# Second layer's products in column halves, behind the first layer's and in a projection bank, with two score banks in the last stage

## What is computed

```python
# layer 0: 20 heads of 64
n = layer_norm(x);  x = x + attention(n, n, a1)            # self-attention
n = layer_norm(x);  x = x + attention(n, ctx, a2)          # over 77 rows of context
x = geglu_ff(layer_norm(x)) + x
# layer 1: 20 heads of 8; text = ctx[:, :-4], ip = ctx[:, -4:]
q = heads(x @ W_q)
probs_t  = softmax(q @ heads(text @ W_k).T * s)            # 128 x 73 a head
text_out = probs_t @ heads(text @ W_v)
qsem  = l2norm(probs_t @ text);  sem = qsem @ l2norm(ip).T
fused = q @ heads(ip @ W_k_ip).T * s + 0.5 * sem
ip_out = (softmax(fused) * fside) @ heads(ip @ W_v_ip)
out = (text_out + ip_out) @ W_out + b_out + x
```

## Time and profile before

| | us |
|---|---|
| runs shown | 3484.98 median, 3480.99 to 3485.95 |
| the profiled execution | 3485.28 |
| its span | 3483.4 |
| TensorE, matmuls busy | 3335.4 (96%) |
| TensorE, weight loads busy | 3131.8 (90%) |
| DVE busy | 2438.3 (70%) |
| ACT busy | 2314.2 (66%) |
| POOL busy | 1329.5 (38%) |

### The profile page before, as it was taken

The page is one execution under the profiler, slowest core; times in us unless marked ns, Lnnn a source line. Parts: engine busy times, 40 slices in busy tenths (PEclk is TensorE's granted clock), DMA queues, the critical chain, the costliest instruction groups (busy, mean ns, idle before and its releaser), DMA issues. The chain is left out here.

```text
span 3483.4 us, 96098 instructions
## 1 busy us (share of the span) xinstructions
PE 3335.4 (96%) x34878; PEld 3131.8 (90%) x34878; DVE 2438.3 (70%) x7677; ACT 2314.2 (66%) x6485; POOL 1329.5 (38%) x1657
## 2 busy tenths in 40 slices
PE   5899999999999999999999999999999999999997
PEld 4789999999899999999999899998999999899987
DVE  6657677767767767677767767767677776777655
ACT  4566676766767676676766767676676766767654
POOL 2223343333434433343433434433343333434333
PEclk9999999999999999999999999999999999999998
DMA  6432324223142332324223142332324223142310
GB/s 157 157 116 69 105 63 126 74 86 103 54 123 70 108 90 68 108 63 122 78 83 105 54 123 68 106 94 63 113 64 118 82 82 106 54 124 68 94 51 11
DMA packets 210732, 313.84 MB, mean 90 GB/s; under 512 B 31232, under 2 KB 167520, under 8 KB 210272
## 3 DMA queue, kind: packets, MB, share of 16 engines
q1 hardware_dynamic: 209984, 307.53, 30.5%
q10 hardware_dynamic: 288, 0.16, 0.0%
HBM read 267.97 MB, written 14.42 MB: 81 GB/s over the span
## 5 line engine op out<-in xcount | busy, mean ns | idle before, releaser
L997 ACT ACTIVATE SE<-PS,mx 128x77 f32<-128x77 f32 (+1 forms) x2560 | 674.8, 355 | 271.9 <-DVE mx L1248 271.2
L1461 POOL TENSOR_TENSOR SE<-SE,rs 128x512 f32<-128x512 f32 (+1 forms) x640 | 552.7, 869 | 625.7 <-DVE rs L1270 625.7
L1454 POOL TENSOR_TENSOR n<-qq,p_half 128x4 f32<-128x4 f32 x320 | 327.4, 1023 | 987.0 <-DVE qq L1299 987.0
L1265 DVE TENSOR_REDUCE sums<-SE 128x4 f32<-128x512 f32 (+1 forms) x640 | 368.3, 576 | 217.8 <-ACT SE L997 217.3
L985 ACT ACTIVATE PTs<-PT 128x1024 f32<-128x1024 f32 (+1 forms) x320 | 326.5, 1020 | 242.3 <-PE PT L811 240.7
L933 ACT ACTIVATE qk<-PG 128x512 f32<-128x512 f32 (+1 forms) x640 | 326.3, 510 | 127.2 <-PE PG L612 125.5
L773 PE MATMUL PW<-w_o,OTs 128*128 128x160 f32 x2560 | 408.8, 303 | 0.0
L1248 DVE TENSOR_REDUCE mx<-PS 128x8 f32<-128x1024 f32 (+1 forms) x320 | 323.0, 1010 | 115.6 <-PE PS L793 113.4
L827 PE MATMUL PV<-PTs,v_sb 128*64 128x128 f32 (+1 forms) x5120 | 351.1, 279 | 12.3 <-DVE SE L1291 12.0
L773 PEld LDWEIGHTS PW<-w_o,OTs 128*128 128x128 f32 x2560 | 359.7, 191 | 0.0
L876 PE MATMUL PV<-later 73*128 73x86 f32 x2560 | 331.0, 272 | 2.3 <-ACT later L1006 1.4
(11 more groups left out here) (209 smaller groups left out, 8439.1 us busy)
## 6 DMA issues: line engine op xcount, KB each, us to landing
q_slice<-q_split SPq DMA_DIRECT2D x630, 192.0 KB, 2.4
vc_slice<-vc_split SPq DMA_DIRECT2D x155, 512.0 KB, 4.0
kc_slice<-kc_split SPq DMA_DIRECT2D x150, 256.0 KB, 2.9
q1st<-q_hi SPq DMA_DIRECT2D x320, 32.0 KB, 2.1
k1st<-k_hi SPq DMA_DIRECT2D x160, 38.5 KB, 2.2
xres<-in_x_dram SPq DMA_DIRECT2D x32, 160.0 KB, 2.7
q1st<-q_lo SPq DMA_DIRECT2D x160, 32.0 KB, 2.1
out_dram<-x SPq DMA_DIRECT2D x64, 80.0 KB, 1.6
```

Source lines behind the costliest of these rows:

```text
L997: last = a_(SE[:, n % 4, J * i:J * i + J], PS[:, e, J * at:J * at + J], ACT.Exp, bias=mx[:, q % 2, 4 * e + at:4 * e + at + 1])
L1265: v.tensor_reduce(sums[:, n % 2, :], SE[:, n % 4, 0:4 * J].rearrange("p (i j) -> p i j", j=J), AX, ALU.add)\
L1454: gp.tensor_tensor(n20[:, b % 2, 4 * w:4 * w + 4], qq[:, b % 2, 4 * w:4 * w + 4], p_half[:, 0:4], ALU.pow)\
L1461: gp.tensor_tensor(e, e, rs[:, n % 2, :].unsqueeze(2).to_broadcast([128, 4, J]), ALU.mult)\
```

## The change

Four things are changed together. The products of a unit (`probs_v1`) are split in two halves of 64 rows of output, so that 4 matmuls of 128 columns of weights become 8 of 64, written to partitions 0 to 63 and 64 to 127. They are no longer issued in part 2 of the beat behind the unit, but in part 0 of the beat after that, directly behind `probs_v`. They no longer go to `PV` but are a job, `pv1`, first in its step, with a bank of `PG` that `unit_out` frees; the semaphore `pv1_done` goes, and `probs_v` and `probs_v1` don't wait for each other's readers. `unit_out` moves on DVE from the end of the beat to sub 0 behind `softmax_in`, `unit_norms` from there to sub 1 behind the first `prob_sums`, `norms_of` on POOL to sub 1 behind the normalisations. The tail's steps start one step later and its jobs stand at the same steps as before. In the last stage (`alone`) the scores of every second unit go to a bank of `PS`, and the scores are issued ahead of the transposes.

```diff
-    TAIL_JOB = {"ipT": 7, "ip": 10, "oT1": 13, "y": 16}
+    TAIL_JOB = {"ipT": 6, "ip": 9, "oT1": 12, "y": 15}
...
-            return 3 * l1_beat(g, W1 * b + W1 - 1) + 7
+            return 3 * l1_beat(g, W1 * b + W1 - 1) + 8
+
+        def alone(g, k):
+            return l1_beat(g, k) > DUOS * GROUPS + 1
+
+        def scores1_bank(g, k):
+            return PS[:, 0, :] if alone(g, k) and k % 2 else PT[:, 1, :]
...
+            unit = l1_at(t // 3 - 2) if t % 3 == 0 else None
+            products1 = [("pv1",) + unit] if unit else []
...
-            return first + v, [x for x in late_at(t) if x[0] != "v"]
+            return products1 + first + v, [x for x in late_at(t) if x[0] != "v"]
...
-                        "ctx1": "gv_done", "ipT": "ipT_done", ...
+                        "ctx1": "gv_done", "pv1": "on_done", "ipT": "ipT_done", ...
...
 # probs_v
-                    if product1[0]:
-                        pe.wait_ge(S["on_done"], product1[0])
 # scores1
-                    if j > 1:
+                    if alone(g, k - 1):
+                        pe.wait_ge(S["exp1_done"], j - 2)
+                        pe.wait_ge(S["exp_done"], NL0 * GROUPS)
+                    elif j > 1:
                         pe.wait_ge(S["exp1_done"], j - 1)
...
-                    mm(PT[:, 1, 0:4 * T], q1st[...],
+                    mm(scores1_bank(g, k)[:, 0:4 * T], q1st[...],
...
 # probs_v1
+                    name = ("pv1", g, k)
+                    pe.wait_ge(*read_out(JOBS[JOB[name] - len(PG)]))
                     pe.wait_ge(S["pts1_done"], j)
-                    if multiplied:
-                        pe.wait_ge(S["ots_done"], multiplied)
-                    if j > 1:
-                        pe.wait_ge(S["on_done"], j - 1)
...
-                        last = mm(PV[:, GV * i + off:GV * i + off + GS + D1], PTs1[0:TT, 128 * i:128 * i + 128],
-                                  gv[:, b % 2, 2 * w + i // 2, off:off + GS + D1], start=True, stop=True)
-                    last.then_inc(S["pv1_done"], 1)
-                    product1[0] = j
+                        for c in range(2):
+                            last = mm(bank(name)[64 * c:64 * c + 64, GV * i + off:GV * i + off + GS + D1],
+                                      PTs1[0:TT, 128 * i + 64 * c:128 * i + 64 * c + 64],
+                                      gv[:, b % 2, 2 * w + i // 2, off:off + GS + D1], start=True, stop=True)
+                    last.then_inc(S["job_full"], 1)
...
 # TensorE's steps
                         if duo_at(beat - 1):
                             probs_v(*duo_at(beat - 1))
+                        if l1_at(beat - 2):
+                            probs_v1(*l1_at(beat - 2))
+                    ahead = part == 1 and l1_at(beat) and alone(*l1_at(beat))
+                    if ahead:
+                        scores1(*l1_at(beat), turned)
                     if part == 1 and l1_at(beat - 1):
                         probs_transposed1(*l1_at(beat - 1), turned)
-                    if part == 1 and l1_at(beat):
+                    if part == 1 and l1_at(beat) and not ahead:
                         scores1(*l1_at(beat), turned)
...
-                    if part == 2 and l1_at(beat - 1):
-                        probs_v1(*l1_at(beat - 1), multiplied)
...
 # DVE's steps
                     if sub == 0 and l1_at(beat - 2):
-                        unit_norms(*l1_at(beat - 2))
+                        unit_out(*l1_at(beat - 2))
...
                         prob_sums(g, 2 * d)
+                    if sub == 1 and l1_at(beat - 2):
+                        unit_norms(*l1_at(beat - 2))
...
-                    if sub == 2 and l1_at(beat - 1):
-                        unit_out(*l1_at(beat - 1))
...
 # POOL's steps
-                    if sub == 0 and l1_at(beat - 2):
+                    if sub == 1 and l1_at(beat - 2):
                         norms_of(*l1_at(beat - 2))
```

More of the change, by code:

```diff
@@ L462, in read_out @@
                         "down": "down_added", "q1": "q1_done", "k1": "k1_done", "vip": "vip_done",
-                        "ctx1": "gv_done", "ipT": "ipT_done", "ip": "o1_done", "oT1": "o1T_done", "y": "y_done"}
+                        "ctx1": "gv_done", "pv1": "on_done", "ipT": "ipT_done", "ip": "o1_done", "oT1": "o1T_done", "y": "y_done"}
             return S[freed_by[name[0]]], NTH[name]
@@ L485, in wait_gv_used @@
                 if g0 >= 0:
-                    engine.wait_ge(S["pv1_done"], l1_count(g0, W1 * b0 + W1 - 1))
+                    engine.wait_ge(S["job_full"], JOB[("pv1", g0, W1 * b0 + W1 - 1)] + 1)
             @block.sync
@@ L875, in probs_v1 @@
                         off = D1 * (i % 2)
[L876 to L879 removed]
+                        for c in range(2):
[3 more added lines that the diff above has]
+                    last.then_inc(S["job_full"], 1)
                 for t in range(FIRST, LAST):
                     beat, part = divmod(t, 3)
[L883 removed]
+                    turned = min(max(beat + 1, 0), DUOS * GROUPS)
                     if part == 0:
@@ L890, in _ @@
                             probs_v(*duo_at(beat - 1))
+                        if l1_at(beat - 2):
[3 more added lines that the diff above has]
+                        scores1(*l1_at(beat), turned)
                     if part == 1 and l1_at(beat - 1):
                         probs_transposed1(*l1_at(beat - 1), turned)
-                    if part == 1 and l1_at(beat):
+                    if part == 1 and l1_at(beat) and not ahead:
                         scores1(*l1_at(beat), turned)
                     for name in jobs_at(t)[0]:
-                        job(name)
+                        if name[0] != "pv1":
+                            job(name)
                     if part == 1 and beat > DUOS * GROUPS and l1_at(beat):
                         keep_busy(6)
-                    if part == 2 and l1_at(beat - 1):
-                        probs_v1(*l1_at(beat - 1), multiplied)
                     for name in late_at(t):
@@ L1004, in pt1_out @@
                     if j > 1:
-                        act.wait_ge(S["pv1_done"], j - 1)
+                        act.wait_ge(S["job_full"], JOB[("pv1",) + divmod(j - 2, GB * W1)] + 1)
                     a_(PTs1[0:TT, :], PT[0:TT, 0, :], ACT.Copy).then_inc(S["pts1_done"], 1)
@@ L1014, in exp1 @@
                     for i in range(4):
-                        last = a_(SE1[:, j % 2, TT * i:TT * i + TT], PT[:, 1, T * i:T * i + TT], ACT.Exp,
+                        last = a_(SE1[:, j % 2, TT * i:TT * i + TT], scores1_bank(g, k)[:, T * i:T * i + TT], ACT.Exp,
                                   bias=mx1[:, j % 2, i:i + 1])
@@ L1274, in unit_out @@
                     j = l1_count(g, n)
-                    dve.wait_ge(S["pv1_done"], j)
+                    ps = take(("pv1", g, n))
                     b, w = n // W1, n % W1
-                    o = PV[:, 0:4 * GV].rearrange("p (i d) -> p i d", d=GV)
+                    o = ps[:, 0:4 * GV].rearrange("p (i d) -> p i d", d=GV)
                     r = rr[:, b % 2, 4 * w:4 * w + 4]
```

12 lines of the change are left out of this document (6 added, 6 removed).

## The result

The changed kernel takes 3604.12 us (median of 4 runs, 3601.84 to 3604.97) against 3485.17 in the same comparison: ratio 1.0343, 95% interval 1.0325 to 1.0361. It is slower by 3.4%. The forecast was 3595 with a range of 3500 to 3670, and 0.84 on slower.

A forecast was written before the change was run, and what follows sets the result against it. TensorE looked like the bound, but its waits on ACT and DVE were only just covered. Terms summed to +7.8 us a group, +115 over 296 beats, +110 with the last stage: 3485 to 3595 us, range 3500 to 3670.

The forecast's parts named there:

- The signs that the prediction named: 16 loads in about 0.7, 75 kc waits of about 0.6 or more, ACT waiting, L677 later, TensorE about 92% busy.
- The products: On TensorE, column halves cut a unit from 0.90 to 0.62 us, gaining 0.28; bounds 0.55 to 0.87 a unit.
- The rival that has load and stream in turn: Loads don't overlap streams in one row group: 1.03 us a unit, 3715 us in all; chance 0.03.
- ScalarE: In beats with transposes of x, ACT reads the later qk products later, delaying transposes: +1.85 us a group.
- VectorE and kc: Beats 8 to 12: kc waits for unit_out to free its bank, and unit_norms delays DVE's copy of v: +4.15 a group.
- The price of unit_norms: On DVE, unit_norms moved behind the first prob_sums adds 0.45 us, net 0.42, ahead of later copies.
- Sums: Beats 1, 6 and 16, with sums of a normalisation on DVE: copy of v later, +1.95 us a group.
- The rest: Beat 18 +0.5, beat 3 -0.4, beat 0 -0.25, beats 13 and 15 about 0 us.
- The last stage: Last 22 second-layer beats: second score bank lets exp run earlier, less added costs: -5 us, bounds -15 and +5.
- third rival: The tiles don't gain: 0.87 us a unit, 0.25 more on both sides, 3665 us in all; chance 0.06.
- TensorE is the bound and takes its gain: Bank waits hide because DVE or ACT catch up: 83 us saved over 296 beats, 3400 us; chance 0.12.

The follow-up runs named there:

- the old places: Changed kernel with the last stage's products, unit_out and norms back where the kernel before issues them: 3602.73 us, ratio 1.0337 to the kernel before.
- x7: Changed kernel with three orders together: kc products later, ScalarE's eviction ahead of its reading, second layer's products first: 3463.46 us, 0.9931 of the kernel before.

## Why the prediction was right, and where it was not

The span grew by 119.1 us: 111.3 in the 296 beats (forecast 115), 14.4 in the tail (forecast -5), and -6.6 ahead of the 296 beats (forecast 0). The last is no effect of the change: that start took 262.3 us in the profile after and 269.6 in the kernel with one score bank, which is the same program up to there. So the loss in the beats was forecast with its mechanism. That the total came within 9 us of it owes something to luck: the tail was missed by 19 us, and the terms within a group cancel (-0.5 on the sums, +0.35 on the rest).

The signs that the prediction named came: 16 loads in 0.70 at the new place, 75 waits of 0.55 to 0.57 before the kc load behind unit_out, ScalarE idle before its first reading, the transposes late behind an idle TensorE, and TensorE busy 92%.

- **The products.** Forecast 0.62 a unit and 0.28 less. The trace has 16 loads in 0.70 in beat 2 and in 0.64 where the products stand first, qk 0.60 later in the beat, and undone they cost 0.30 more. The rival that has load and stream in turn would need over 1.0 a unit, and falls. The Trainium skill (TensorE: Matmul & The Clock Gate, Part 3) states that LDWEIGHTS overlaps with in-flight MATMULs only when row_grp differs. This case's trace does not agree: both halves take the same 73 rows, and their 16 loads and matmuls need 0.64 to 0.70.
- **ScalarE.** Beats with transposes: forecast +1.85 a group, measured +1.76. Beat 2 was to lose 0.5 by 0.51 on the second reading: it lost 0.48, and the second reading ends 0.49 later. The eviction moved ahead gave exactly that back, so the mechanism is shown for beats 2, 7 and 18.
- **VectorE and kc.** Forecast +4.15 (its terms add to 4.17), measured +4.20; in beat 8 +1.58 against +1.62. The kc load was to be 1.20 later and is 1.24. That unit_out's start is the lever is shown by the products put first. The price of unit_norms, 0.42 net, is shown in part: moved in the kernel before, it costs 0.37 in beat 8 and as much in beat 9, and nothing in beats 10 to 12. What it costs there behind unit_out, where the slack may be gone, no run tells.
- **Sums.** Forecast +1.95, measured +1.43 (0.45, 0.46, 0.52). This term was sized too high. It leaned on unit_norms too, and on its own that costs nothing in beats 1, 6 and 16.
- **The rest.** Beat 18 +0.15 instead of +0.5, beat 3 -0.55 instead of -0.4, and beats 0 and 15 +0.29 and +0.37 instead of -0.25 and 0. The step that failed in these two is that the image's steps, one part later, were priced at nothing: with norms and steps moved and no product, beats 0 and 15 have +0.93 and +0.37, and with the norms alone nothing. Sum of all: +7.6 against +7.8 a group.
- **The last stage.** The step that failed is "I take -5". It rested on the second bank letting exp run earlier; removing the bank changes nothing. My next theory, that the late products make the chain, is not borne out by the old places. What stands in the rows is a lower granted clock. Over all thirteen profiled kernels here (x7 left out) the tail is 121.8 to 142.1 us and its mean clock 0.89 to 0.76, and the product of the two stays between 107 and 118. Whether the clock is the cause or the sign of a TensorE that waits more is open. Both kernels already issue six matmuls in each beat of the last stage whose results nothing reads (`keep_busy`); more of them would tell, and this was not tried. A rival in the schedule stands too: the images' steps, one part later. The tail is 125.3 with the norms moved alone and 133.7 with these steps as well (127.8 before), and every kernel with a tail over 136 has them. No run moves the steps by themselves.
- **Readings and sums.** The prediction takes the 214 us of the earlier trace rows for the second layer alone, but nine beats of the first layer start in them, and the tail is 127.8 us. Its third rival adds to 3669, not 3665. Neither moves the forecast.

The rival "TensorE is the bound and takes its gain" is at most half true of a neighbouring kernel: with the products put first and two more orders changed, the 296 beats are 43 us shorter than before, of the 83 that it named. Whether these are the halves' gain is not shown: no run undoes the halves there or gives the kernel before the same orders.

## What to carry to other kernels

When work moves forward in a beat, count what each reader of its result, and each reader of what it pushed back, does next; here TensorE was saved 0.28 a unit, and for it the transposes came 0.5 later in a beat that ScalarE holds and the kc load 1.2 later in one that VectorE holds. An operation whose reader is next in the queue of a busy engine belongs ahead of one whose reader is occupied anyway: issuing two groups of products in the other order gave 83 us. Where two waits end together, an experiment that takes one away can show nothing, so try both at once before calling a wait harmless.

## What the hardware showed that was not expected

- Column halves paid only beside other column halves: 0.30 a unit next to L827, and nothing (-0.04 to +0.06 a beat) between matmuls of the whole array, where the two edges together cost 0.33.
- The granted clock of the tail differs by kernel where the other engines have the same work: 0.79 after and 0.89 with the halves alone, whose tail is the shortest of all, 121.8 us.
- One execution of the three orders took 10814 us. The other engines' work is nearly as always (VectorE 2476.8 us, 2409.1 in the changed kernel), but its profile has matmuls 2 to 3 times as long (L782, the output projection, 796 ns on average where the other kernels have about 300). It shows the granted clock as 1.00 from start to end, also in the first 100 us, where the kernel before has 0.90 and the one after 0.88; it may hold no record of the clock, so the clock is not ruled out. The other executions of the same kernel took 3457 to 3464. No run here explains it.
